# Second layer between batches: eight token roundings on VectorE, in one row or in four pairs among the row maxima

## The reference

```python
def act_quant(x):
    s = 127.0 / jnp.clip(jnp.max(jnp.abs(x), axis=-1, keepdims=True), EPS)
    return jnp.clip(jnp.round(x * s), -128, 127) / s
qkv = act_quant(adaln(x, c, g1, ...)) @ weight_quant(w_qkv).T + b_qkv
attn = softmax(q @ k.T * hd ** -0.5);  o = attn @ v
x = x + act_quant(o) @ weight_quant(w_proj).T + b_proj
```

## Time and profile before

| | |
|---|---|
| median of 3 runs | 2795.2 us (2794.4 to 2797.38) |
| the profiled execution's own time | 2797.68 us |
| span of its trace | 2795.9 us |
| TensorE busy in matmuls | 2621.9 us (94%) |
| VectorE busy | 2162.2 us (77%) |
| GpSimd busy | 1964.9 us (70%) |
| ScalarE busy | 1830.6 us (65%) |
| VectorE's rounding, line 1919 | 32 operations, about 0.43 us each |

### The profile page before, as it was taken

The page is one execution under the profiler, slowest core; times in us unless marked ns, Lnnn a source line. Parts: engine busy times, 40 slices in busy tenths (PEclk is TensorE's granted clock), DMA queues, the critical chain, the costliest instruction groups (busy, mean ns, idle before and its releaser), DMA issues. The chain is left out here.

```text
span 2795.9 us, 59973 instructions
## 1 busy us (share of the span) xinstructions
PE 2621.9 (94%) x21716; PEld 1469.8 (53%) x21761; DVE 2162.2 (77%) x4455; ACT 1830.6 (65%) x3302; POOL 1964.9 (70%) x1579
## 2 busy tenths in 40 slices
PE   7899989999999999999959998999899989987998
PEld 5655566554665547655425554555455445543443
DVE  5777768777687777877667778777877787768997
ACT  4366664665656655566656677667766776667996
POOL 0298844897449873598748986988798778965542
PEclk9999999999999999999979999999999999999999
DMA  6122343224432244323232313321432132245444
GB/s 234 39 58 59 125 135 121 58 62 152 125 103 59 60 146 139 97 62 92 85 81 50 84 41 106 81 59 32 118 81 59 35 108 58 62 156 185 109 102 109
DMA packets 168764, 260.42 MB, mean 93 GB/s; under 512 B 85388, under 2 KB 91668, under 8 KB 167576
## 3 DMA queue, kind: packets, MB, share of 16 engines
q1 hardware_dynamic: 166680, 250.27, 32.7%
q0 software_dynamic: 1792, 6.33, 0.6%
HBM read 99.15 MB, written 38.88 MB: 49 GB/s over the span
## 5 line engine op out<-in xcount | busy, mean ns | idle before, releaser
L547 DVE TENSOR_REDUCE a_mxs<-ps 128x1 f32<-128x512 f32 x2048 | 1268.2, 681 | 258.7 <-PE ps L414 256.3
L508 ACT ACTIVATE a_p<-ps 128x512 f32<-128x512 f32 x2048 | 1043.5, 606 | 205.1 <-PE ps L428 194.8
L368 POOL TENSOR_TENSOR a_sum<-a_p 128x512 f32<-128x512 f32 x736 | 939.0, 1285 | 204.2 <-PE ps L448 114.5
L414 PE MATMUL ps<-a_k,a_q 96*128 96x512 f32 x2048 | 854.8, 424 | 25.3 <-DVE a_mxs L547 21.0
L428 PE MATMUL ps<-a_q,a_k 98*128 98x512 f32 x2048 | 808.7, 419 | 15.7 <-ACT a_p L508 9.8
L448 PE MATMUL ps<-a_sum,a_unit 128*32 128x512 f32 x1536 | 650.5, 596 | 0.6 <-POOL a_sum L368 0.6
L374 POOL TENSOR_TENSOR a_sum<-a_sum,a_p 128x512 f32<-128x512 f32 x480 | 618.4, 1288 | 37.6
L448 PE MATMUL ps<-a_p,xv 128*32 128x512 f32 x3968 | 639.0, 595 | 0.0
L414 PEld LDWEIGHTS ps<-a_k,a_q 96*128 96x128 f32 x2048 | 389.7, 190 | 259.7 <-DVE a_mxs L547 105.5
L428 PEld LDWEIGHTS ps<-a_q,a_k 98*128 98x128 f32 x2048 | 384.2, 189 | 242.3 <-ACT a_p L508 144.7
L517 ACT ACTIVATE a_ots<-ps 128x512 f32<-128x512 f32 x256 | 152.6, 598 | 403.5 <-PE ps L448 402.5
(11 more groups left out here) (250 smaller groups left out, 3103.9 us busy)
## 6 DMA issues: line engine op xcount, KB each, us to landing
a_q<-qh SPq DMA_DIRECT2D x256, 128.0 KB, 2.3
a_k<-kh SPq DMA_DIRECT2D x256, 128.0 KB, 2.4
a_q<-ql SPq DMA_DIRECT2D x128, 128.0 KB, 2.4
a_k<-kl SPq DMA_DIRECT2D x128, 128.0 KB, 2.4
x<-a_p SPq DMA_DIRECT2D x64, 256.0 KB, 2.1
a_p<-in_w_fc SPq DMA_DIRECT2D x12, 1024.0 KB, 8.0
kh<-in_x SPq DMA_DIRECT2D x4, 2048.0 KB, 14.6
a_p<-x SPq DMA_DIRECT2D x16, 512.0 KB, 5.9
```

Source lines behind the costliest of these rows:

```text
L368: pair = pool.tensor_tensor(tile, keys[0], keys[1], ALU.add)
L414: pe.matmul(self.mx[self.mx_ring[at]], self.q[j][0:96, t * P:(t + 1) * P], self.k[j][0:96, half * HALF:(half + 1) * HALF], start=True, sto ...
L508: act.activation(self.key_tile(u, kt), self.st[self.st_ring[CHUNKS * k + n]], ACT.Exp, scale=self.scale).then_inc(self.s_exp, 1)
L547: dve.reduce_max(self.mxs[:, k % 2, c:c + 1], self.mx[self.mx_ring[CHUNKS * k + c]], axis=AX.X).then_inc(self.s_mxr, 1)
```

## The change

The roundings of tokens no longer stand eight in a row behind QK10. A table gives four places: tiles 0 and 1 behind QK10, 2 and 3 behind V5, 4 and 5 behind V6, 6 and 7 behind V7, in each case ahead of the two reductions that stand there. The roundings after the last batch stay where they were (they stand ahead of the list there).

```diff
--- before.py
+++ after.py
@@ -1640,6 +1640,7 @@
             return [(kind, n, banks[i % len(banks)], order[i - len(banks)] if i >= len(banks) else None,
                      chunks.index((kind, n)) if (kind, n) in chunks else None) for i, (kind, n) in enumerate(order)]
         MT, MROW = 9, 11
+        BITS = {("QK", EARLY + 2): (0, 1), ("V", LEAD): (2, 3), ("V", LEAD + 1): (4, 5), ("V", LEAD + 2): (6, 7)}
 
         NEXT_ONLY, BOTH, TAIL_ONLY = products(True, False), products(True, True), products(False, True)
 
@@ -1984,8 +1985,8 @@
                             dequantized(kind, n, ps[:, bank, :], nxt, tail)
                             if kind == "QK" and 0 < n <= EARLY and tail is None:
                                 low(n - 1, nxt)
-                        if (kind, n) == ("QK", EARLY + 2) and tail is not None:
-                            for t in range(TT):
+                        if tail is not None and nxt is not None:
+                            for t in BITS.get((kind, n), ()):
                                 eight_bits(tail, t)
                         if part is not None:
                             att.prelude_dve(dve, nxt, part)
```

## The result

| | before | changed |
|---|---|---|
| median, 12 runs each | 2794.92 us | 2802.63 us |
| lowest to highest | 2791.78 to 2800.56 | 2797.26 to 2806.04 |
| ratio of the runs | | 1.0026, 95% interval 1.0018 to 1.0034 |
| the profiled execution | 2797.68 | 2797.26 |

The change makes the kernel slower by 0.26%, some 7 us. A comparison of the two spans would show nothing. So all times from here on are counted from the first rounding of their change of batch, and lengths of a batch from one first rounding to the next.

What follows compares the result with a forecast made beforehand. TensorE bounds attention; ScalarE's squares bound its start, GpSimd 0.8 us behind. Per change of batch 0.3 + 1.5 - 0.5 = 1.3, taken as 1.2; 2795.2 + 3.6 = 2798.8 us, range 2793.5 to 2803.0.

Steps and rivals of the forecast that it cites:

- (e): TensorE's 4.3 us idle ahead of the fourth score lowers its clock; 1.2 us lost per change of batch, late exponential included.
- (a): VectorE's own rounding work: four pairs take 3.48 us against 4.05 for eight in a row, 0.57 us less.
- (b): TensorE's 4.25 us idle in the list and the slow clock behind it go; QK11's scaling 3.16 us earlier.
- (c): Eighth rounding 3.06 us later, GpSimd waiting for it; its last low part ends at 1739.98 for 1738.48.
- (d): Next attention's first exponential 0.8 us later, GpSimd the bound; only 0.3 us left if TensorE keeps its clock.
- come back as the ring lets TensorE run ahead again: In the head, part of the low-clock loss regained by ScalarE's pace: about 5 x 0.1, taken as 0.5 us.
- my 1.5: In the head, 5.2 us at low clock make 6.0 matmul pairs in place of 8.5: 1.5 us behind.
- Rival 1: Same change with TensorE's clock kept or soon back: 3 x 0.3 = +0.9 us, 2796.1; chance 0.22.
- Rival 2: Low clock wholly in the head, late exponentials not absorbed: 2.0 to 2.6 us each, about 2802; chance 0.21.
- Rival 3: GpSimd's chain doesn't hold the exponential: fully passed -9.5 us, 2785.7; chance of more than 0.2% faster 0.07.
- the 3.16 us: How much earlier QK11's scaling was to come in VectorE's list with pairs, per change of batch.
- Rival 4: TensorE's clock falls in the list all the same: +1.8 us each, 2800.6; shares the main forecast's chance, 0.50.

Runs made afterwards that it cites:

- Run 9: Changed kernel with roundings in two fours and unneeded matmuls filling TensorE's pauses (8 and 5 in the list, 7 in the head): 2794.02 us, ratio 0.9984.
- run 10: Changed kernel, GpSimd's V3 and V4 biases ahead of its rounding wait, residual biases first behind it, 7 unneeded matmuls in the head's pause: 2790.94 us, 0.9978.
- run 11: Changed kernel with two fours, V3 and V4 biases ahead of GpSimd's wait, residual biases first behind it, all TensorE pauses filled: 2789.86 us, 0.9974.
- run 2: Changed kernel with 16 unneeded matmuls keeping TensorE busy ahead of the fourth score: 2798.76 us, ratio 1.0008 to the kernel before.
- run 7: Changed kernel without GpSimd's wait for the eighth rounding, 7 unneeded matmuls in TensorE's pause ahead of the fourth score: 2792.16 us, ratio 0.9995.
- run 8: Changed kernel without GpSimd's wait for the eighth rounding, its residual biases moved ahead of those of V5 to V7: 2809.87 us, ratio 1.0056.
- run 3: Kernel before (eight roundings in a row) with 16 unneeded matmuls filling TensorE's 4.25 us idle in the list: 2787.91 us, ratio 0.9979.
- run 5: Changed kernel without GpSimd's wait for the eighth rounding ahead of the biases of V3 to V7: 2796.41 us, ratio 0.9997.
- run 4: Changed kernel with roundings in two fours, behind QK10 and behind V5, in place of pairs: 2795.88 us, ratio 0.9997.
- run 6: Kernel before (eight in a row) without GpSimd's wait for the eighth rounding: 2798.41 us, ratio 1.0014.
- run 1: Changed kernel once more, no edit, for a second trace: 2802.75 us, ratio 1.0022 to the kernel before.

## Why the prediction was right and where it was not

The range held (2793.5 to 2803.0, measured 2802.63), by 0.4 us; the likeliest time, 2798.8, was 3.8 us low. Within 0.2% had the highest chance, 0.72, where 0.26% slower was measured, with an interval that lies clear of no change. The path to the loss was right, and its size was too small in two terms: (e), and the last batch, which the sum had at nothing. That the range still held is luck in part, since it had no room set aside for the second. By the steps:

- (a) and (b), VectorE's list. Right: QK11 8.25 us (8.36 worked out), Y0's sum 22.63 (22.73), first score 27.93 (28.1), clock 1.00 in the list. Of the idle in the list some was left, 1.05 us behind the first pair, where I had at most 0.9.
- (c) the eighth rounding and GpSimd. Right: 7.13 us (7.22), wait 12.6 us (12.7), V biases without a gap, last low part 33.13 (33.26). Run 9's series shows the chain, and runs 10 and 11 that shortening it takes the loss away.
- (d) the first exponential 33.16 us (33.33), 0.6 us late (0.8). That 0.3 us of it are left if the clock holds is what run 2 measured, 40.48 for 40.17.
- (e) the pause and the clock. The mechanism was right: an idle of 4.23 us (4.3), a low clock behind it in all six places, and run 2 shows it as cause. **The size was off.** I let 0.5 us "come back as the ring lets TensorE run ahead again" and took 1.2 us per change of batch. In the six places the loss was 1.1 to 2.1 us, 1.6 in the mean, with 5.1 us of low clock behind the pause in the mean, against the 5.2 that I had. Less the 0.3 us of run 2, 1.3 us are left of my 1.5: what comes back is 0.2 us and not 0.5, and the rounding from 1.3 down to 1.2 had no ground. VectorE's maxima at 0.61 us set the pace as soon as the clock is back. 3 x 1.6 makes 4.8, not 3.6.
- The rest, from 4.8 to the 7.3 us that the ratio makes (its interval reaches from 5.0 to 9.5), lies for the most part behind the last first rounding, where the prediction had only "the fourth row of eight, after the last batch, stays". In both kernels TensorE is idle for 4.57 us ahead of the transposes there. In the kernel before the clock was then low for 6.8 us; in the changed kernel's trace for 13.7 us, so that the last projection ran at half speed for most of its way. The changed kernel:

```profile
2502.60:2516.30 13.70, 9.23 (x43) 5.08 (x45) 4.83 (x10) 9.04 (x14) 8.99 (x8) 0.50 0.61 242
2511.91 9.00 PE L1784 MATMUL ps<-a_next_wp,tok 128*128 128x512 bf16 x31 [1.77 <-ACT tok L1839]
```

  The projection in the kernel before:

```profile
2513.81 6.85 PE L1783 MATMUL ps<-a_next_wp,tok 128*128 128x512 bf16 x31 [1.61 <-ACT tok L1838]
```

  The last residual sum ends 16.9 us behind the first rounding in the kernel before, 19.2 and 19.3 us in the two traces of the changed one: 2.3 to 2.4 us, and 4.8 + 2.3 makes 7.1. The instructions are the same. The other traces fall into the same kinds: the low clock lasts 13.7 us in seven of the thirteen (all three of pairs with the wait, runs 7, 8, 10 and 11), 10.2 in two (runs 3 and 5) and 6.8 in four (before, runs 4, 6 and 9). In the seven the last residual sum ends at 19.0 to 19.4 us, in the other six at 16.9. To the end of the program that stretch takes 290.7 to 294.2 us. Why the low clock lasts longer there in the changed kernel, and whether it does so in every execution, no run shows; two traces are few. Over whole executions run 1 lists a granted clock of 0.9752 in the mean of eleven and 0.9766 for the kernel before in 33, which makes some 8 us more of low clock (an estimate: 2 x 0.0014 x 2800), though the changes of batch hold no more of it than before (17 and 20.5 us in the two traces, for 20.5).
- One of the two traces has 1.5 us more in the last batch's attention, with a low clock at 2496.3. Low stretches in the same region stand in the traces of runs 4, 9 and 11, but not in that of the kernel before. Whether the changed kernel meets them more often stays open too.

Rival 1 was right in its price (0.3) and wrong in its condition. Rival 2, with a chance of 0.21, has the measured total in its span (+6.0 to +7.8, measured +7.3 to +7.7), but not by its condition: the loss per head passed 1.9 us in two of six places only, and the total is made up by the last batch. Rival 3, that the 3.16 us pass through, fell: with GpSimd's chain behind the eighth rounding, none of it did. Rival 4 did not occur in the changed kernel's two traces, nor in run 2, though it did in run 5, with the same pairs.

The Trainium skill, TensorE: Matmul & The Clock Gate, Part 1, by which the slow clock is the default and activity is what releases it, was the reason that I kept (e) in the sum. The traces agree: the idle of 4.23 us was followed by a low clock, and so were idles of 2.12 us (run 4).

## What to carry to other kernels

Spreading a block of work so that a busy engine waits less helps only if nobody waits for the last piece of the block: look who waits for the end of it, here an engine with 26 us of work behind that wait and 0.8 us of slack. A wait of TensorE that is taken away in one place and stands up again in front of its critical stretch costs more there, as the low clock then falls on work that bounds the kernel; filling the pause with products that nobody reads settled it both times (runs 2 and 3). A stretch whose instructions did not change can still change its time through the clock, so follow it to the program's end before a sum is closed. Before a wait between VectorE and GpSimd is dropped, find out whether it keeps apart operations that block each other.

## What the runs showed of the hardware that was not expected

- VectorE's TENSOR_SCALAR from SBUF to SBUF stands still while GpSimd adds: 1.02 and 1.19 us for 0.17 (run 7), 1.3 to 1.5 for 0.43 a rounding (run 8), while reductions and scalings out of PSUM beside GpSimd keep their 0.68 us. The Trainium skill, SBUF — State Buffer, Who interferes with whom, says that of GpSimd and a VectorE instruction in a two-port mode, which a tensor_scalar can enter, the first to start keeps the shared ports for its whole instruction and the other is blocked in full; the rows above agree, VectorE's two small operations ending with GpSimd's additions.
- TensorE's clock fell to 0.50 to 0.54 behind idles of 2.12 us in all three places of run 4. Behind the idle of 1.05 us in the pairs it held in all nine places of the changed kernel, run 1 and run 2, and fell in four of the nine of runs 5, 7 and 10. In three of these four, in runs 5 and 7, TensorE had stood idle for another 1.06 us some 2.7 us before; in the fourth, in run 10, there was only the 0.45 us of the next pair between.
- A low clock of TensorE costs a stretch that VectorE paces too: about 0.25 us for each us of it, as a pair of matmuls at 0.86 us is slower than a maximum at 0.61.
- Without an instruction changed, and behind the same idle of 4.57 us, TensorE's clock stayed low for 6.8, 10.2 or 13.7 us in different traces, and the last residual sum came at 19.0 to 19.4 us behind the first rounding where it lasted 13.7, at 16.9 in all the others.
